# Attention outputs gathered and divided by DMA instead of transposed, maxima rows sent from GpSimd, a narrower causal mask

## The reference, cut to what matters

```
x = ln(x + banded self attention block(x))        # 8 heads of 32, a band of 64 keys each side
x = ln(x + causal cross attention(x, ctx))        # 16 heads of 16
x = ln(x + lora feed-forward(x))
x = ln(x + (softmax(q k^T / 4) v) @ fc_w^T + fc_b + x)      # 16 heads of 16, all 2048 keys
x = ln(x + (softmax(q k^T / 4 + mask) v) @ Wo + bo)         # 16 heads of 16, all 1601 keys
x = ln(x + two of eight experts(x))
```

## Time and profile before

| | |
|---|---|
| median of 3 runs | 3195.89 us (3194.34 to 3197.38) |
| the profiled execution | 3194.37 us, its span 3192.6 us, mean granted clock 0.937 |
| a0 `attend` | 85 to 262 us of the span |
| x0 `attend` | 540 to 952 us |
| decoder stage, all pairs | 1315 to 2716 us |
| its last closing, to the next block | 2716 to about 2731 us |
| PE, DVE, ACT, POOL busy | 2810.0, 2065.5, 1568.0, 223.8 us |

### The profile page before, as it was taken

The page is one execution under the profiler, slowest core; times in us unless marked ns, Lnnn a source line. Parts: engine busy times, 40 slices in busy tenths (PEclk is TensorE's granted clock), DMA queues, the critical chain, the costliest instruction groups (busy, mean ns, idle before and its releaser), DMA issues. The chain is left out here.

```text
span 3192.6 us, 83730 instructions
## 1 busy us (share of the span) xinstructions
PE 2810.0 (88%) x34974; PEld 1425.7 (45%) x34975; DVE 2065.5 (65%) x4240; ACT 1568.0 (49%) x2122; POOL 223.8 (7%) x295
## 2 busy tenths in 40 slices
PE   6686987999996997799999999999999999379992
PEld 3474552444544563144434343443433343246661
DVE  3345137888845236688999898988898985312224
ACT  2222322666662322266777776776776768023331
POOL 2001201000000002300000000000000000210003
PEclk9888997999997999699999999999999999589996
DMA  5412033011001004312112212111111110710012
GB/s 155 119 43 94 1 91 91 3 39 39 3 2 37 1 0 126 88 41 64 45 43 51 60 34 55 44 44 54 43 45 44 44 44 2 257 45 31 31 33 87
DMA packets 112871, 173.46 MB, mean 54 GB/s; under 512 B 17882, under 2 KB 88427, under 8 KB 112147
## 3 DMA queue, kind: packets, MB, share of 16 engines
q1 hardware_dynamic: 109460, 160.11, 17.4%
q0 software_dynamic: 3072, 8.39, 0.8%
HBM read 127.63 MB, written 40.51 MB: 53 GB/s over the span
## 5 line engine op out<-in xcount | busy, mean ns | idle before, releaser
L1304 DVE TENSOR_REDUCE d_part_max<-d_ps_m 128x1 f32<-128x512 f32 (+1 forms) x1964 | 1128.0, 631 | 93.5 <-PE d_ps_m L1291 57.0
L1612 ACT ACTIVATE d_prob<-d_ps_s 128x1024 f32<-128x1024 f32 x928 | 898.8, 1021 | 347.8 <-PE d_ps_s L1481 341.0
L1291 PE MATMUL d_ps_m<-k_st,q_st 97*32 97x512 bf16 (+1 forms) x5296 | 482.0, 363 | 19.4 <-DVE d_part_max L1304 15.9
L1481 PE MATMUL d_ps_s<-q_st,k_st 98*32 98x512 bf16 x5104 | 441.8, 383 | 9.8 <-ACT d_prob L1612 8.4
L690 DVE TENSOR_REDUCE x_part_max<-x_att_ps_m 128x1 f32<-128x512 f32 (+2 forms) x578 | 309.4, 586 | 50.4 <-PE x_att_ps_m L675 22.7
L936 ACT ACTIVATE x_att_prob<-x_att_ps_s 128x1024 f32<-128x1024 f32 (+3 forms) x296 | 258.7, 921 | 140.7 <-PE x_att_ps_s L817 84.6
L1499 PE MATMUL d_ps_o<-d_prob,a_values 128*32 128x512 f32 x2048 | 267.7, 596 | 0.0
L1291 PEld LDWEIGHTS d_ps_m<-k_st,q_st 97*32 97x32 bf16 x5296 | 142.9, 96 | 273.5 <-DVE d_part_max L1304 128.0
L1291 PE MATMUL d_ps_m<-q_st 97*32 97x512 bf16 (+1 forms) x2560 | 232.1, 361 | 2.3 <-DVE d_part_max L1304 0.4
L1481 PEld LDWEIGHTS d_ps_s<-q_st,k_st 98*32 98x32 bf16 x5104 | 138.5, 97 | 195.2 <-issue 83.2
L1499 PE MATMUL d_ps_o<-d_prob,x_values 128*32 128x512 f32 x1664 | 215.5, 593 | 0.4 <-ACT d_prob L1612 0.4
(11 more groups left out here) (326 smaller groups left out, 3329.1 us busy)
## 6 DMA issues: line engine op xcount, KB each, us to landing
k_st<-parts_k SPq DMA_DIRECT2D x90, 256.0 KB, 5.6
k_st<-parts_k SPq DMA_DIRECT2D x90, 208.0 KB, 4.3
l_w<-in_l_w SPq DMA_DIRECT2D x16, 1024.0 KB, 11.7
q_st<-parts_q SPq DMA_DIRECT2D x48, 256.0 KB, 4.7
q_st<-parts_q SPq DMA_DIRECT2D x192, 64.0 KB
q_st<-parts_k SPq DMA_DIRECT2D x30, 256.0 KB
q_st<-parts_k SPq DMA_DIRECT2D x30, 208.0 KB
parts_q<-a_proj_parts SPq DMA_DIRECT2D x16, 384.0 KB, 2.5
```

Of the source, the lines that this page charges most:

```text
L1291: mm = pe.matmul(bank[q:q + COLUMNS, 0:w], self.query(s, h, ROW_MASK + 1, a * P + q, COLUMNS), self.key(s, h, ROW_MASK + 1, k, w), start=T ...
L1304: dve.tensor_reduce(self.part[:, h * QT + a, i:i + 1], bank[:, 0:w], AX.X, ALU.max).then_inc(s_read, 1)
L1481: mm = pe.matmul(ps_s[u][k:k + COLUMNS, hh, :], maxima.key(s, h, ROW_MAX + 1, kt * P + k, COLUMNS), maxima.query(s, h, ROW_MAX + 1, 0, QC) ...
L1612: act.activation(prob[:, p % 2, 2 * u:2 * u + 2, :], ps_s[u][:, :, :], ACT.Exp, scale=scale).then_inc(s_prob, 1)
```

## The change

- **Output path of the decoder stage.** `turn_out`, `turn_tokens`, `copy_tokens` and `normalise` go, with `o_tok` and `inv_den`. `o_fm` now holds a chunk's output with features on partitions (two halves of 128, two chunks deep). For each step, SP issues `gather(s)` after `copy_o`: per head one DMA of 16 rows of 512 from `o_raw` to `o_fm`, and one DMA that lays the head's row of 512 sums on 16 partitions of 32 (`sums`); 8 DMAs a step, placed in SP's order at the first pair of the next step, in front of that pair's stack loads. A half is two steps. `invert(half)` on DVE, two pairs on, takes the reciprocal of `sums` (128 by 32). `spread(half)` on SP, four pairs on, writes it to DRAM (`inverses`), waits for that, and reads it back in 8 broadcast DMAs, so that each head's 512 inverses stand on its 16 partitions of `den`. `divide(half)` on DVE, ten pairs on, multiplies `o_fm` (128 by 512). For the last half the sums are laid out in full at once, `invert` runs on 128 by 512, and no DRAM is passed.
- `copy_o(s)` waits for the gathers of the step before, where it waited for `turn_out`. The closing tasks of a chunk start at the tenth pair instead of the second, one pair shorter.
- **Quarter products.** `out_product`, `unit_product` and `v_product` are done in quarters of 32 columns of the array.
- **Rows of maxima in `attend`.** They are sent by GpSimd, after its two copies of values (`v_grp`) for the group; SP keeps the stack loads. Rows that `project` sends stay on SP and have a semaphore of their own (`s_early`). SP waits for the last values product before what is `behind` (in a0, clearing `x_slots`).
- **Narrow mask.** The causal mask's matmul covers the last 128 columns of a block only.

```diff
-            off = QC - P
-            select(c["causal_q"][:, :], ALU.is_ge, NEG, off, [[-1, QC]], 1)
+            select(c["causal_q"][:, :], ALU.is_ge, NEG, 0, [[-1, P]], 1)
...
-                m = cst["causal_q"][:, QC - w:QC]
+                m, edge = cst["causal_q"][:, :], bank[:, w - P:w]
             for q in range(0, P, COLUMNS):
-                mm = pe.matmul(out[q:q + COLUMNS, :], cst["ident_bf"][:, q:q + COLUMNS], m, start=False, stop=True,
+                mm = pe.matmul(edge[q:q + COLUMNS, :], cst["ident_bf"][:, q:q + COLUMNS], m, start=False, stop=True,
...
         @block.sync
-            def group(g, stream, last):
-                if not last:
-                    sp.wait_ge(s_load, 16 * LOADS * (g + 1))
-                    sp.wait_ge(s_pv, 2 + pairs_before(g, 0))
-                    load_stacks(sp, at, g + 1, slot(g + 1), q_st, k_st, parts_q, parts_k, s_load)
-                for (dg, c), x in stream.turn_at.items():
-                    maxima.send(sp, slot(g + dg), c, s_mred, entries_before(g) + x + 1)
+            with sp.Fori(0, NG - 1) as g:
+                sp.wait_ge(s_load, 16 * LOADS * (g + 1))
+                sp.wait_ge(s_pv, 2 + pairs_before(g, 0))
+                load_stacks(sp, at, g + 1, slot(g + 1), q_st, k_st, parts_q, parts_k, s_load)
+            sp.wait_ge(s_pv, 2 + pairs_before(NG, 0))
             behind(sp)
...
+                for (dg, c), x in stream.turn_at.items():
+                    maxima.send(pool, maxima.s_sent, slot(g + dg), c, s_mred, entries_before(g) + x + 1)
...
-    TURN_AT = 2
+    GATHERED_AT = 2
+    SPREAD_AT = 4
+    DIVIDED_AT = 10
...
+            def gather(s):
+                half = half_of(s)
+                k, m = half // DT, half % DT
+                sp.wait_ge(s_ocopy, s + 1)
+                if half >= 1:
+                    sp.wait_ge(s_kept if half < plan.halves - 1 else s_norm,
+                               16 * half if half < plan.halves - 1 else half)
+                if k >= 2:
+                    sp.wait_ge(s_prod, QT * (k - 1))
+                for j in range(GH):
+                    first = (s % (NG // DT) * GH + j) * SH
+                    rows = slice(first, first + SH)
+                    row = o_raw[32 * j + SH:32 * j + SH + 1, :]
+                    if half < plan.halves - 1:
+                        sp.dma_start(sums[rows, :], row.rearrange("p (r n) -> p r n", r=SH)).then_inc(s_gather, 16)
+                    else:
+                        sp.dma_start(den[rows, :], row.rearrange("p (o n) -> p o n", o=1)
+                                     .to_broadcast((1, SH, QC))).then_inc(s_gather, 16)
+                    sp.dma_start(o_fm[rows, k % 2, m, :], o_raw[32 * j:32 * j + SH, :]).then_inc(s_gather, 16)
+
+            def spread(half):
+                sp.wait_ge(s_inv_den, half + 1)
+                sp.dma_start(inverses[half].rearrange("(p n) -> p n", p=P), sums[:, :]).then_inc(s_kept, 16)
+                sp.wait_ge(s_kept, 16 * (half + 1))
+                if half >= 1:
+                    sp.wait_ge(s_norm, half)
+                for j in range(P // SH):
+                    sp.dma_start(den[j * SH:(j + 1) * SH, :], inverses[half:half + 1, j * QC:(j + 1) * QC]
+                                 .to_broadcast((SH, QC))).then_inc(s_spread, 16)
...
                 for m in range(DT):
-                    mm = pe.matmul(plan.bank(step)[:, 0:D], o_fm[:, n % 2, m, :],
-                                   wo_sb[:, plan.chunks[k][0], m, :], start=(m == 0), stop=(m == DT - 1))
+                    for q in range(0, P, COLUMNS):
+                        start = a * P + q
+                        mm = pe.matmul(plan.bank(step)[q:q + COLUMNS, 0:D],
+                                       o_fm[:, k % 2, m, start:start + COLUMNS],
+                                       wo_sb[:, plan.chunks[k][0], m, :], start=(m == 0), stop=(m == DT - 1),
+                                       skip_group_check=True)
...
-                    act.wait_ge(s_turn, s)
+                    act.wait_ge(s_gather, 16 * 2 * GH * s)
...
+            def invert(half):
+                dve.wait_ge(s_gather, 16 * 2 * GH * (NG // DT) * (half + 1))
+                some = sums if half < plan.halves - 1 else den
+                dve.reciprocal(some[:, :], some[:, :]).then_inc(s_inv_den, 1)
+
+            def divide(half):
+                k, m = half // DT, half % DT
+                if half < plan.halves - 1:
+                    dve.wait_ge(s_spread, 16 * (P // SH) * (half + 1))
+                dve.wait_ge(s_inv_den, half + 1)
+                dve.tensor_tensor(o_fm[:, k % 2, m, :], o_fm[:, k % 2, m, :], den[:, :], ALU.mult).then_inc(s_norm, 1)
```

More of the change, by code:

```diff
@@ L1435, in _ @@
                         maxima.send(sp, s, s_mred, x - plan.ahead + 1)
+                for s in range(len(plan.steps)):
+                    if plan.first[s + 1] == p:
+                        gather(s)
                 for s in range(2, len(plan.steps)):
@@ L1438, in _ @@
                         load(s)
+                for half in range(plan.halves - 1):
+                    if plan.spread_at[half] == p:
+                        spread(half)
                 for task in plan.tasks[p]:
@@ L1557, in unit_product @@
                 for d in range(DT):
[L1558 to L1559 removed]
+                    for q in range(0, P, COLUMNS):
+                        start = m * P + q
+                        mm = pe.matmul(plan.bank(step)[q:q + COLUMNS, 0:n],
+                                       w_sb[:, 0 if side == "q" else 1, d, start:start + COLUMNS],
+                                       src[:, d, k:k + n], start=(d == 0), stop=(d == DT - 1), skip_group_check=True)
                 mm.then_inc(s_mm, 1)
@@ L1783, in _ @@
                         reductions(place)
-                for s in range(len(plan.steps)):
-                    if plan.out_at[s] == p:
-                        normalise(s)
+                for half in range(plan.halves):
+                    if plan.gathered_at[half] == p:
+                        invert(half)
+                for half in range(plan.halves):
+                    if plan.divided_at[half] == p:
+                        divide(half)
                 for task in plan.tasks[p]:
```

147 lines of the change are left out of this document (53 added, 94 removed).

## The result

The changed kernel takes 3167.72 us (median of 4 runs, 3162.30 to 3172.91) against 3196.14 us of the kernel before, a ratio of 0.9911 with a 95% interval of 0.9889 to 0.9933: 28 us faster. The forecast was 3127 us, in a range of 3092 to 3165. The sign was right, the size was off by 41 us, and the median lies outside the range.

What follows compares the result with a forecast made beforehand. PE was taken to set the decoder's pace, DVE close behind, and DMA waits to hold a0. a0 -34, x0 +10 - 11, project -1, decoder -48 + 9 + 6 made -69: 3127 us, range 3092 to 3165.

Steps and rivals of the forecast that it cites:

- a0: In this stage's `attend`, maxima rows sent by GpSimd: waits -26.6, clock -7.5, together -34 us; bounds -20 and -44.
- x0: In this stage's `attend`, GpSimd's rows cost +10 us (bounds 0 and +20) and the narrow mask saves 11.
- The wait of `invert`: Decoder: DVE waits about 1.2 us for gathers in 15 halves; banks hide part, 0.6 a half, +9 us.
- What PE is spared in the decoder: Decoder: `turn_out` removed -21.4 us, products in quarters -18.9, `turn_tokens` beside them -8; sum -48.
- The quarters: Decoder: out, unit and value products in quarters of the array spare PE 0.31 us each, 61 products, -18.9 us.
- Rival B: Decoder: DVE sets the pace once PE is lighter, the 48 us come down to about 12; 3163 us, chance 0.10.
- rival A: GpSimd's rows queue behind the stack loads and a0's wait stays; only -35 us, 3161 us, chance 0.12.
- the load that is late next: In a0, the stack load: 3 us come back as a wait in two groups, 1.5 in the first.
- the clock: -7.5 counted: In a0, shorter waits leave less time at half speed: 7.5 us saved, counted from 3 x 3.
- The mask: Narrow causal mask: -11 us in `attend`, -1 in `project`; bounds 0 and -15.5.
- The tail: Decoder's end: first out product 8.2 us later, the four products' quicker pace returns 2; +6 us.

Runs made afterwards that it cites:

- e1: The kernel before with only GpSimd's sends of maxima rows and the narrow mask, nothing of the decoder's change: 3162.69 us, ratio 0.9903.
- e2: The changed kernel with the reciprocal of the gathered sums at the third pair instead of the second: 3145.02 us, ratio 0.9849.
- e9: e3 and e8 together, with a shorter tail (ScalarE issues four DMAs, last reciprocal and division in four pieces): 3125.95 us, ratio 0.9788.
- e12: e9 with the division back on DVE: 3126.86 us, ratio 0.9793.
- e4: The kernel before with the quarter products alone: 3187.32 us, ratio 0.9981.
- e10: e2 with the three products on the full array again instead of in quarters: 3156.05 us, ratio 0.9875.
- e3: e2 with the division of 15 halves moved from DVE to GpSimd: 3138.82 us, ratio 0.9836.
- e5: e2 with an extra, unread DVE product in four pairs each of two steps of every decoder chunk: 3160.46 us, one run.
- e7: e3 with the scaling of closed rows moved from DVE to GpSimd for all chunks but the last: 3134.62 us, ratio 0.9832.
- e8: e2 with the stack loads of a0's next group cut in two by columns: 3134.34 us, ratio 0.9829.

## Why the forecast was right in sign and wrong in size

**Order of the argument.** Reading a0 by its waits and costing the decoder by PE's blocks gave the right sign, since a0 and x0 alone carried it (e1). The decoder, from which half of the gain was to come, gave none in the changed kernel. Four terms of the sum were mis-sized.

**The wait of `invert`** is the step that failed most plainly: "of which three banks let PE run on: I take 0.6 a half, +9", with a bound of +18. The length of the wait was well forecast (1.2 us; measured 18.9 / 15 = 1.26). But the banks covered a quarter of it in the first attention and none in the second, and the cost was 23 us (e2), 5 of them for the clock that fell behind the three longest (3 x 3.4 us at half speed). The 3 us by which e2's pairs gained more are lows elsewhere, and such lows come and go between kernels that hardly differ (e9, e12). The gathers themselves came nearly as forecast: the last of a step landed 6.4 to 8.2 us after the copy, 6.9 in the middle, against 6.6.

**What PE is spared in the decoder**, -48. The step that failed is the price: with "PE sets the pace, DVE follows close", every microsecond spared on PE was to shorten the pairs by one. Freed of the wait, the pairs of e2 are 26.3 us shorter than before. By parts: `turn_out` was right, a plain step went from 36.64 to 35.99, 0.65 against 0.69. The quarters brought 8 to 9 instead of 18.9 (e4, e10): the price of a block was right, the 57 products in the pairs spare about 16, and PE's microsecond is worth half of one there. `turn_tokens` brought little or nothing instead of 8: 20 us for `turn_out` (31 x 0.65) and 8.6 for the quarters, less the 6.5 that the division costs (e3), are 22 of the 26.3, 1 is the clock's, and 3 are left for it and all else. The residual sums of successive tiles, in the kernel before (with a turn and a full product in each pair) and in e2 (a quarter product alone), on DVE, show it:

```profile
2433.31 0.42 DVE L1739 TENSOR_TENSOR x_tok<-x_tok,d_ps_m 128x256 f32<-128x256 f32 x1
2437.14 0.42 DVE L1739 TENSOR_TENSOR x_tok<-x_tok,d_ps_m 128x256 f32<-128x256 f32 x1 [0.36 <-PE d_ps_m L1532]
2441.45 0.42 DVE L1739 TENSOR_TENSOR x_tok<-x_tok,d_ps_m 128x256 f32<-128x256 f32 x1 [0.35 <-PE d_ps_m L1532]
```

```profile
2406.29 0.42 DVE L1751 TENSOR_TENSOR x_tok<-x_tok,d_ps_m 128x256 f32<-128x256 f32 x1 [0.20 <-PE d_ps_m L1556]
2410.44 0.42 DVE L1751 TENSOR_TENSOR x_tok<-x_tok,d_ps_m 128x256 f32<-128x256 f32 x1 [0.20 <-PE d_ps_m L1556]
```

Such a pair takes 3.83 and 4.31 us before and 4.15 after, though PE has some 0.5 us less to do in it: DVE's own 1.03 us for the tile's sum and statistics stand between the reductions on which PE's banks wait. This reason is argued from such waits as the 0.29 us before e2's out product above; no run takes the 1.03 us away. Against these gains, 1.04 us of division and reciprocal in one step of a half cost 0.37 where I had counted nothing (by e3, all of it the division's), perhaps because the 1.34 us that they replace had been spread over both steps and they stand in one. Rival B had this mechanism in part, with a price too high: it left 12 of the 48 us, 26 were left. What the forecast held against it, that DVE has "some 3 us of slack" in a step of 13 pairs, was wrong: 2.73 us added there cost 2.4 (e5). But DVE doesn't set the pace alone either: 1.6 us taken off it beside the closing work brought nothing (e7).

**a0**, -34: -15.4. The eight kernels with this a0 took 148.4 to 154.4 us in it, so the gain is 15 to 21 us and the changed kernel's profile shows it near its least. The waits were to fall from 35.6 to 9 us and fell to 18.0 (4.9 for rows, 13.1 for loads). The rows of maxima were forecast to land 1.9 us after the issue; in x0 they did so in about 1.1, but in a0's first group in 6.4, which is between the stack loads issued beside it (at 98.80, landed at 104.99, and at 99.77, landed at 106.25). So what rival A said of the engines is partly true: this row did not pass the loads already issued. It did pass those that SP had yet to issue, and that is most of the gain. By the Trainium skill (DMA: Bandwidth & Descriptors, SWDGE vs HWDGE vs iDMA), which the forecast had set against rival A, an engine takes turns between its software and its hardware queues. Had that brought the row forward, it would have landed ahead of the loads issued beside it; this group's trace does not bear that out. The larger miss is the load that is late next: I let 3 us come back in each of two groups, and PE waited 7.0 and 6.1. The forecast put PE's first use at about 154.5, 13.0 us after the group's first load was issued, and didn't work out when the last load is there: in the kernel before it landed at 159.13, which makes 4.6 us. In the changed kernel PE was there 11.4 us after the first load, 1.6 sooner, and the last load landed 18.4 us after it, 0.8 later: 7.0 in all. e8 confirms it from the other side. Last, the clock: -7.5 counted, about 0 gained. PE's busy time in the stage is 131 us in both, since in the kernel before most of the low clock had fallen on time in which PE stood still: it was busy in 18.0 of 42.0 us at 0.50, and in 17.9 of 24.6 in the changed one.

**x0**: the rows cost nothing instead of +10. GpSimd's plain DMA takes 0.51 us against the 1.26 that I took from an indirect one; here the nearest row was of another kind, and SP's 0.59 would have been the better guide. The mask brought 10 of the 11 us forecast for it in this stage.

**The tail** was nearly right, +8.9 against +6 (+6.5 beside the second profile of the kernel before): the first product comes 8.5 us later (forecast 8.2), with a reciprocal of 3.35 us (3.4); the 2 us that a quicker pace of the products should return did not come: they follow each other after 1.7 us where it was 1.8 before, with the clock at 0.50 for most of them (and at 1.00 before).

**Sum.** Instead of -34, -1, -39 and +6 the stages gave -15, -10, 0 and +9; some 4 us came from the experts, unforeseen. That is -21 in the profiled executions and -28 in the medians.

## What to carry to other kernels

Where two engines feed each other through a few banks and both are busy over 85%, take a microsecond saved on PE at about half its length, and a wait put in front of the other engine at three quarters of its length to a little more than all of it, with the clock's fall on top; adding the same small work to one engine and then to the other prices both in two runs. A wait that is removed uncovers the one behind it: find out at what time the engine comes to that next operand once the first wait is gone, and compare it with the time at which the operand lands. Put the first reader of a small gather one pair further back than the sum says: being too early by 1.3 us in 15 places cost 23 us here, and standing a pair further back cost nothing that e2 shows.

## What the runs showed of the hardware

- TensorE's clock fell to its lower level for 3.4 us behind the gather waits of 1.73, 1.97 and 2.61 us, and behind none of 1.55 or less, in a stream in which PE was otherwise busy; of waits of 1.3 to 1.9 us for ScalarE, it fell behind some and not behind others. In the steps of the second attention such a fall costs 1.6 us on top of the wait (42.93 us with one, 41.35 without, in e7).
- A plain DMA of 1 KB from GpSimd's queue takes 0.51 to 0.54 us of that engine (the first of a0 0.72) and is there about 1.1 us later on nearly idle DMA engines (share 0.02); with stack loads under way on them it took 6.4 us. An indirect one had taken 0.96 us and 0.30 idle.
- DVE's reciprocal takes 0.35 us for 32 elements a partition, 0.95 for 128 and 3.35 for 512: 6.3 ns an element. A product of 128 by 512 takes 0.69 us on DVE and 1.29 on GpSimd.
- A square root between exponentials costs ScalarE two table loads of 1.28 us, one before the root and one behind it, 2.9 us in all with the root's 0.30 (e9, 2410.66 to 2413.57), and PE stands 1.32 us for it in the second attention. The Trainium skill (ScalarE: Activation LUTs, What ACT_TABLE_LOAD costs) has 1283 ns for it, which the trace bears out, and 1380 ns of drain beside it, which does not show here: in e9 each load starts 0.02 us behind the instruction before it, and the exponential 0.02 us behind the load.
